# Block stores at a register's address in place of GpSimd scatters, for the first of four edge streams of a graph network

## The chip, the cores and the metric

One Trainium2 chip, one of its cores. The metric is the device time of one execution in microseconds (us), the median of several runs.

## The reference

Two layers of a relational graph convolution over 50,000 nodes of 128 features and 50,000 edges of 8 types, with `dst` sorted. Cut to what matters:

```python
h = relu(layernorm(x))
for l in range(2):
    m = relu(h[src] + edge_attr)                       # one message per edge
    seg = etype * n + dst
    mean = segment_sum(m, seg) / max(count(seg), 1)    # per (type, node)
    out = einsum('rnd,rdo->no', mean, weight[l])       # summed over the 8 types
    out = out + h @ root[l] + bias[l]
    h = batch_norm(out, gamma[l], beta[l])
    if l == 0: h = relu(h)
return x + h
```

`dst` is drawn as 50000 times the square of a uniform number and then sorted, so that the first edges lie close together in their nodes: the first quarter of the edges ends near node 3125.

## The kernel before

**Tiles, groups, streams.** The 50,000 edges, in order of dst, are cut into NT = 394 tiles of 127 edges. NG = 99 groups hold up to H = 4 tiles each, tile t belonging to group t % 99: stream 0 is tiles 0 to 98, stream 1 tiles 99 to 197 and so on. One group is one step of the edge loop, and there is one edge loop per layer.

**One step, group g.** GpSimd (POOL) gathers `h[src]` for each tile (`gather`, L759) into a ring of 20 groups (layer 0) or 9 (layer 1). VectorE (DVE) normalises it together with ScalarE (ACT) in layer 0, or scales it in layer 1, and adds the edge rows, which SyncE (SP) has loaded into `xb`, a ring of XB = 4 groups (`edge_rows`, L638; `edge_sum`, L1061 and L1067). TensorE (PE) transposes the tile (L1456) and spreads the edge types (L1463); ACT writes the message (L1265); DVE splits it by type (`by_type`, L1078); PE multiplies by the weights (`products`, L1481 and L1482, 8 products per tile); ACT copies the product (L1273); PE sums the edges of one node (`node_sums`, L1493); ACT copies the sums to `ob`, a ring of OB = 4 groups (`sums_out`, L1294), and row 0 of the sums to the next tile's input (`carry`, L1286). A tile's last node may go on in the next tile, so the sums of it are carried there.

**The scatters.** POOL writes each tile of `ob` to the table `acc[l]` in DRAM with an indirect DMA of 128 rows (`scatter`, L770). The row numbers are in `idx_t`; rows that hold no node's sum go to spare rows behind the table. Scatters and gathers alternate on POOL: `gathers_before` gives how many gathers lie ahead of the n-th scatter, 80 ahead in layer 0 and 36 in layer 1 at the start, 28 at the end. The first scatter of a group waits for `ob_ready` of that group. ACT waits for the scatters of group g-4 before it overwrites their slot of `ob`. When `dst` isn't sorted, a flag found during the set-up sends POOL, PE and DVE into a branch that works one scatter at a time; it isn't taken here.

**Order on the other queues.** PE's iteration i holds products(i), with types(i+2), turn(i+2) and node_sums(i-1) after its second tile. In layer 1, 44 of the iterations also hold four transposes (`first_rows`, L1503) and a product (`first_product`, L1508) of whole chunks of node rows, whose results are used after the loop. SP's iteration n loads the edge rows of group n, and in layer 0 loads and stores half chunks of normalised rows (L663, L652) and zeroes a part of `acc[1]` (L670); in layer 1, at n = 4i+2, it waits for the transposes of two chunks before (`ownT_ps`) and loads the next whole chunk (`table_dma`, L531). At the end of a layer, POOL adds three joined rows (`join_streams`, L795) once all scatters have landed, and SP then loads the sums chunk by chunk.

**Set-up.** DVE works out from `dst` and the types: whether dst is sorted (`falls`, `flag_i`), the scatter rows (`idx_t`), the slot of each edge's sum in its tile (`slot`, later `ikey_t`) and the inverse counts. ACT zeroes `acc[0]` meanwhile.

Of the kernel before, what the change touches and what calls it, by code (L numbers as in the profile page):

```python
# [41 lines left out]
def gnn_kernel(nc, x, src, dst, edge_attr, edge_type, weight, root, bias, gamma, beta, out):  # L42
# [70 lines left out]
    def tiles(g):  # L113
        return [s * NG + g for s in range(H) if s * NG + g < NT]

    ORDER = [(g, t) for g in range(NG) for t in tiles(g)]
    assert sorted(t for g, t in ORDER) == list(range(NT)) and tiles(0) == [s * NG for s in range(H)]

# [5 lines left out]
    with ctx:  # L124
# [48 lines left out]
        falls = sb("falls", [P, 1])  # L173
        goes_on = sb("goes_on", [P, NB])

        J = H - 1
# [139 lines left out]
        def own_at(i):  # L316
            return own_place[OWN_FIRST[i]]
# [134 lines left out]
        xb_in = [sem(f"xb_in{s}") for s in range(XB)]  # L452
        scat_out = [sem(f"scat_out{s}") for s in range(OB)]
        ve_ready = sem("ve_ready")
        sd_ready = sem("sd_ready")
# [112 lines left out]
        def tiles_done(gg, ring):  # L568

            return sum(len(tiles(k % NG)) for k in range(gg % ring, gg + 1, ring))  # L570

# [33 lines left out]
        def _(sp):  # L605
# [131 lines left out]
        def _(pool):  # L737
# [24 lines left out]
            def scatter(g, t, l, add):  # L762
                gg = l * NG + g
                if t == g:
                    pool.wait_ge(ob_ready, gg + 1)

                if t // NG == 2 and g + 4 < NG:
                    pool.wait_ge(tr_ps, gg + 5)
                how = {"compute_op": ALU.add, "bounds_check": N - 1, "oob_is_err": False} if add else {}
                pool.indirect_dma_start(out=acc[l], out_offset=at(idx_t[:, t:t + 1]), in_=ob[:, gg % OB, t // NG, :],  # L770
                                        in_offset=None, **how).then_inc(scat_out[gg % OB], 16)

            def scatter_alone(g, t, l):

                gg = l * NG + g
                j = t // NG
                if j > 0:
                    pool.wait_ge(scat_out[gg % OB], 16 * (tiles_done(gg, OB) - len(tiles(g)) + j))
                elif gg > 0:
                    pool.wait_ge(scat_out[(gg - 1) % OB], 16 * tiles_done(gg - 1, OB))  # L780
                scatter(g, t, l, True)

            def gathers_before(n, l):
# [62 lines left out]
        def _(dve):  # L846
# [28 lines left out]
            own.link(v.tensor_tensor_reduce(out=kill[:, :, 1:P], in0=dstf[:, :, 0:T], in1=dstf[:, :, 1:P], scale=1.0, scalar=0.0,  # L875
                                            op0=ALU.subtract, op1=ALU.max, accum_out=falls[:, 0:1]))
            own.link(v.tensor_scalar(falls[:, :], falls[:, :], 0.0, None, ALU.is_gt))
            dve.sem_inc(falls_ready, 1)


# [4 lines left out]
            own.mark(v.memset(agree[:, :, T:P], 0.0))  # L885
            own.mark(v.memset(keep[:, :, 0:1], 0.0))
            own.join()
# [5 lines left out]
            own.link(v.tensor_tensor(keep[:, :, :], kill[:, :, :], keep[:, :, :], ALU.mult))  # L893
            own.mark(v.tensor_tensor(kill[:, :, turned], keep[:, :, :], spare_row[:, :, :], ALU.add))

# [8 lines left out]
            dve.wait_ge(flag_ps, 1)  # L904
            v.tensor_scalar(flag_i[:, :], ps_s[0][0:1, 0:1], 0.5, None, ALU.is_gt).then_inc(flag_ready, 1)
            dve.wait_ge(cols_ps, 3)
# [311 lines left out]
        def _(act):  # L1218
# [426 lines left out]
```

## Time and profile before

| | |
|---|---|
| median of 3 runs | 2535.77 us (2532.77 to 2540.87) |
| span of the profiled execution | 3011.2 us |
| mean granted TensorE clock in it | 0.893 |
| PE, DVE, ACT, POOL busy | 2477.2, 1916.1, 969.3, 1603.3 us |
| edge loop of layer 0 | about 135 to 1309 us of the profiled execution |
| whole-chunk stage and batch norm of layer 0 | about 1310 to 1498 us |
| edge loop of layer 1 | about 1541 to 2745 us |
| stages behind it | about 2750 to 3011 us |

The profile is of one execution, and that one spans 3011.2 us, 475 us more than the median of the timed runs. Its durations are used below, but its total isn't that of a timed run. Times are counted from the span's start. "Idle before, <- X" is the time for which the engine did nothing ahead of the instruction, and X what ended it; "issue" means that the profile shows nothing that it waited for.

### The profile page before, as it was taken

The numbers are of one execution on the slowest core, as the hardware profiler recorded it, in microseconds if no ns is written. First come the engines' busy times: TensorE is split into PE (matmuls) and PEld (weight loads), VectorE is DVE, ScalarE is ACT, GpSimd is POOL, SyncE is SP. The second block draws the span as 40 slices with busy tenths as digits, with TensorE's granted clock in tenths as the row PEclk, the third lists the DMA queues.
The fourth block names the chain that finished last, engine by engine and source line by source line (L and its number), as shares of the span: only waits on it lengthen the run. The fifth ranks groups of instructions, "written<-read, shape, count | busy, mean of one in ns | idle before, by whom it ended". The sixth has DMA issues, their size and how long they took to land. (4 is left out here: it accounts for less than half of the span.)

```text
span 3011.2 us, 50450 instructions
## 1 busy us (share of the span) xinstructions
PE 2477.2 (82%) x19096; PEld 2315.6 (77%) x19096; DVE 1916.1 (64%) x5063; ACT 969.3 (32%) x2076; POOL 1603.3 (53%) x1613
## 2 busy tenths in 40 slices
PE   2388888888888888889968888898988889887976
PEld 1387887888787887789857878787888878777965
DVE  7566776777766667748855555565665556554754
ACT  0233344444444444424311222222222222222555
POOL 7566555665556555520056666666666666663000
PEclk7699998988998999999978999899999999988986
DMA  9533433344433333359922222222222222224889
GB/s 348 197 102 116 137 127 128 128 129 133 133 128 127 128 118 122 113 208 418 371 66 67 63 84 62 85 65 85 65 86 64 85 64 84 78 73 176 312 320 403
DMA packets 241842, 436.67 MB, mean 145 GB/s; under 512 B 39075, under 2 KB 144126, under 8 KB 241596
## 3 DMA queue, kind: packets, MB, share of 16 engines
q1 hardware_dynamic: 166134, 237.95, 22.6%
q0 software_dynamic: 53808, 115.45, 12.5%
q10 hardware_dynamic: 21654, 79.99, 6.6%
q8 instruction: 155, 2.54, 0.3%
q14 instruction: 91, 0.75, 0.1%
HBM read 255.41 MB, written 177.83 MB: 144 GB/s over the span
## 5 line engine op out<-in xcount | busy, mean ns | idle before, releaser
L1481 PE MATMUL ps_y<-arena 128*128 128x128 f32 x11032 | 1517.4, 287 | 227.9 <-issue 200.7
L1481 PEld LDWEIGHTS ps_y<-arena 128*128 128x128 f32 x11032 | 1412.1, 202 | 303.5 <-issue 278.5
L770 POOL DMA_INDIRECT acc<-arena x788 | 776.3, 985 | 728.1 <-ACT arena L1294 448.4
L1078 DVE SCALAR_TENSOR_TENSOR arena<-ps_s,arena 128x512 f32<-128x512 f32 (+1 forms) x1386 | 842.7, 678 | 362.9 <-PE ps_y L1482 186.0
L759 POOL DMA_INDIRECT arena<-h_rows,arena x394 | 411.9, 1045 | 300.3 <-DMA h_rows<-chunk_mem 180.5
L1273 ACT ACTIVATE arena<-ps_y 128x512 f32<-128x512 f32 (+1 forms) x198 | 117.9, 595 | 1259.8 <-remote 953.3
L759 POOL DMA_INDIRECT arena<-in_x_dram,arena x394 | 397.9, 1010 | 126.6 <-issue 118.9
L1482 PE MATMUL ps_y<-arena 128*128 128x128 f32 x1576 | 324.1, 286 | 23.2 <-issue 22.3
L1493 PE MATMUL ps_o<-arena 128*128 128x128 f32 x1576 | 260.8, 303 | 51.6 <-issue 49.0
L1493 PEld LDWEIGHTS ps_o<-arena 128*128 128x128 f32 x1576 | 226.8, 213 | 74.4 <-issue 73.0
L1482 PEld LDWEIGHTS ps_y<-arena 128*128 128x128 f32 x1576 | 254.0, 201 | 29.3 <-issue 29.1
L1265 ACT ACTIVATE arena<-ps_t 128x512 f32<-128x512 f32 (+1 forms) x198 | 115.5, 583 | 416.7 <-remote 310.9
L1090 DVE TENSOR_SCALAR arena<-arena 128x128 f32<-128x128 f32 x788 | 223.9, 352 | 0.0
L1049 DVE RECIPROCAL rstd<-sd 128x8 f32<-128x8 f32 (+2 forms) x99 | 19.6, 198 | 320.7 <-ACT arena L1257 227.2
L1456 PE MATMUL ps_t<-ident,arena 128*128 128x128 f32 x788 | 141.3, 300 | 51.7 <-issue 41.7
L1257 ACT ACTIVATE arena<-arena,nmr,rstd 128x128 f32<-128x128 f32 x394 | 160.8, 477 | 15.3 <-DVE nmr L1050 12.2
L1067 DVE SCALAR_TENSOR_TENSOR arena<-arena 128x512 f32<-128x512 f32 (+1 forms) x99 | 68.2, 689 | 142.6 <-DMA arena<-in_edge_attr_dram 134.5
L1456 PEld LDWEIGHTS ps_t<-ident,arena 128*128 128x128 f32 x788 | 94.8, 155 | 64.3 <-issue 53.8
L1463 PE MATMUL ps_s<-arena 128*128 128x128 bf16 x788 | 90.0, 235 | 37.8 <-issue 36.9
L1294 ACT ACTIVATE arena<-ps_o 128x512 f32<-128x512 f32 (+1 forms) x198 | 116.7, 589 | 2.7 <-PE ps_o L1493 2.7
L1286 ACT ACTIVATE arena<-ps_o 1x512 f32<-1x512 f32 (+1 forms) x196 | 111.4, 568 | 0.0
L1463 PEld LDWEIGHTS ps_s<-arena 128*128 128x128 bf16 x788 | 68.6, 108 | 40.7 <-issue 35.8
(230 smaller groups left out, 2251.7 us busy)
## 6 DMA issues: line engine op xcount, KB each, us to landing
arena<-in_edge_attr_dram SPq DMA_DIRECT2D x190, 256.0 KB
chunk_mem<-acc SPq DMA_DIRECT2D x55, 512.0 KB, 12.3
acc<-arena ACTq DMA_DIRECT2D x28, 896.0 KB
acc<-arena SPq DMA_DIRECT2D x28, 896.0 KB
arena<-in_x_dram SPq DMA_DIRECT2D x45, 512.0 KB, 9.8
arena<-acc SPq DMA_DIRECT2D x43, 512.0 KB, 10.1
chunk_mem<-hn_rows SPq DMA_DIRECT2D x41, 512.0 KB
out_dram<-arena ACTq DMA_DIRECT2D x38, 512.0 KB, 9.4
```

The costliest lines, as they stand in the source:

```text
L759: pool.indirect_dma_start(out=hb[:, hb_slot(gg), t // NG, :], out_offset=None, in_=(x, h1_tab)[l], in_offset=at(src_t[:, t:t + 1])).then_i ...
L770: pool.indirect_dma_start(out=acc[l], out_offset=at(idx_t[:, t:t + 1]), in_=ob[:, gg % OB, t // NG, :], in_offset=None, **how).then_inc(sc ...
L1078: ins = v.scalar_tensor_tensor(mk[:, m, r, 0:n], ps_type[gg % 2][:, 0:n], float(r), mt[:, gg % MT, 0:n], ALU.is_equal, ALU.mult)
L1090: ins = v.tensor_scalar(sm[:, gg % SM, c], iota_f[:, :], ikey_t[:, t:t + 1], inv_t[:, t:t + 1], ALU.is_equal, ALU.mult)
L1257: ins = a_.activation(row, row, ACT.Relu, scale=rstd[:, g % 2, j:j + 1], bias=nmr[:, g % 2, j:j + 1])
L1273: a_.activation(yb[:, gg % 2, 0:w, :].rearrange("p w d -> p (w d)"), ps_y[gg % 2][:, 0:w * D], ACT.Copy).then_inc(yb_ready, 1)
L1294: a_.activation(ob[:, gg % OB, 0:w, :].rearrange("p w d -> p (w d)"), ps_o[gg % 2][:, 0:w * D], ACT.Copy).then_inc(ob_ready, 1)
L1456: last = te.transpose(ps_turn[:, j * D:(j + 1) * D], hb[:, hb_slot(gg), j, :], ident[:, :])
L1463: last = te.matmul(bank[:, j * D:(j + 1) * D], ident_b[:, t % P:t % P + 1].to_broadcast([P, P]), rows_b[:, t // P, :], start=True, stop=True)
L1481: te.matmul(ps_y[gg % 2][:, c], mk[:, gg % MKS[l], r, c], w_sb[l][:, r * D:(r + 1) * D], start=r == 0, stop=False)
L1482: last = te.matmul(ps_y[gg % 2][:, c], mt[:, gg % MT, c], w_sb[l][:, (R - 1) * D:R * D], start=False, stop=True)
L1493: last = te.matmul(ps_o[gg % 2][:, c], sm[:, gg % SM, c], yb[:, gg % 2, j, :], start=True, stop=True)
```

## The change

Tiles 1 to 95 of stream 0 (one in each of the groups 1 to 95) are no longer scattered by POOL. For them the slot of a node's sum in `ob` is its distance from the tile's first node plus 1, and rows without a sum are zero, so that rows 1 to 112 of `ob` are 112 neighbouring rows of the table. SP writes them as one plain DMA, at an address that it loads into a register from `first_i`. A window reaches past its tile's last node and writes zeros there, so the windows go in order: each waits until the one before has landed, and the next window puts the right sums over the zeros. SP issues the window of group n-8 in its iteration n. ACT waits for the window, as it did for the scatter, before it overwrites the slot. The scatter of tile 96 and the join wait for the windows. Set-up gains the slots, the first rows and a test (`over`, `near_end`) that the tiles fit into windows; if not, the one-at-a-time branch is taken.

```diff
+    WROWS = 112
+    SPANS = ((1, NG - 4),)
+    WIDE = [t for a, b in SPANS for t in range(a, b + 1)]
@@ sync
+            def window_rows(g, l):
+                gg = l * NG + g
+                for t in in_window(g):
+                    sp.wait_ge(ob_ready, gg + 1)
+                    if gg > 0:
+                        wait(sp, wide_out, 16 * windows(gg - 1))
+                    first = sp.value_load(first_i[0:1, t:t + 1], min_val=0, max_val=P * (F + 1))
+                    sp.dma_start(acc[l][bass.ds(first, WROWS), :], ob[1:1 + WROWS, gg % OB, t // NG, :]).then_inc(wide_out, 16)
+
+            sp.wait_ge(idx_ready, 1)
             for l in range(L):
+                sp.wait_ge(acc_zero[l], 16 * ZN)
                 for n in range(NG):
                     if l > 0 or n >= 2:
                         edge_rows(n, l)
+                    if n >= 8:
+                        window_rows(n - 8, l)
...
+                for g in range(NG - 8, NG):
+                    window_rows(g, l)
@@ gpsimd, scatter
+                if not add and t in WIDE:
+                    return
+                if not add and t - 1 in WIDE:
+                    pool.wait_ge(wide_out, 16 * windows(gg - 1))
@@ gpsimd, join_streams
+                pool.wait_ge(wide_out, 16 * windows((l + 1) * NG - 1))
@@ vector, set-up
+            t0 = spare_row[:, 0:WB, 0]
+            own.mark(v.tensor_scalar(is_wide[:, :], t0, float(SPARE_ROW + P * SPANS[0][0]), None, ALU.is_ge))
+            own.mark(v.tensor_tensor(over[:, :], dstf[:, 0:WB, T], dstf[:, 0:WB, 0], ALU.subtract))
...
+            near = keep[:, 0:WB, :]
+            own.mark(v.tensor_tensor(agree[:, 0:WB, :], dstf[:, 0:WB, 0:P], dstf[:, 0:WB, T:P].to_broadcast([P, WB, P]),
+                                     ALU.not_equal))
+            own.link(v.tensor_tensor(near, dstf[:, 0:WB, 0:P], dstf[:, 0:WB, 0:1].to_broadcast([P, WB, P]), ALU.subtract))
+            own.link(v.scalar_tensor_tensor(near, near, 1.0, agree[:, 0:WB, :], ALU.add, ALU.mult))
+            own.link(v.tensor_tensor(near, near, slot[:, 0:WB, :], ALU.subtract))
+            for b in range(WB):
+                own.link(v.scalar_tensor_tensor(slot[:, b, :], near[:, b, :], is_wide[:, b:b + 1], slot[:, b, :],
+                                                ALU.mult, ALU.add))
...
+            own.link(v.tensor_scalar(first_i[:, :], dst_t[0:1, 0:WB * P], to_spare[:, 0:1], None, ALU.max))
@@ scalar, sums_out
                     act.wait_ge(scat_out[gg % OB], 16 * tiles_done(gg - OB, OB))
+                    wait(act, wide_out, 16 * windows(gg - OB))
```

## Rows read from the trace of the kernel before

**Rows 1.** The page, part 1: busy time and share by engine.
```profile
PE 2477.2 (82%) x19096; PEld 2315.6 (77%) x19096; DVE 1916.1 (64%) x5063; ACT 969.3 (32%) x2076; POOL 1603.3 (53%) x1613
```
**Rows 2.** Windows of both edge loops: length, busy per engine, granted clock, DMA share, GB/s.
```profile
135.58:1306.82 1171.24, 992.33 (x7788) 949.27 (x7786) 810.59 (x2860) 479.17 (x1190) 689.87 (x702) 0.92 0.37 123
1553.49:2739.33 1185.84, 1043.79 (x8050) 962.54 (x8048) 698.01 (x1350) 256.67 (x477) 760.39 (x746) 0.92 0.25 73
```
**Rows 3.** Timeline (start, length in us), ScalarE: first and last L1273 of the run.
```profile
135.58 0.60 ACT L1273 ACTIVATE arena<-ps_y 128x512 f32<-128x512 f32 x1 [2.88 <-PE ps_y L1482]
...
2739.33 0.49 ACT L1273 ACTIVATE arena<-ps_y 128x384 f32<-128x384 f32 x1 [4.26 <-PE ps_y L1482]
```
**Rows 4.** Timeline, ScalarE, end of layer 1: L1273 of two neighbouring groups.
```profile
2718.04 0.60 ACT L1273 ACTIVATE arena<-ps_y 128x512 f32<-128x512 f32 x1 [3.98 <-PE ps_y L1482]
...
2726.58 0.60 ACT L1273 ACTIVATE arena<-ps_y 128x512 f32<-128x512 f32 x1 [3.90 <-PE ps_y L1482]
```
**Rows 5.** Waits: who waited for whom, us in total, times, longest.
```profile
POOL acc L770 <- ACT arena L1294: 448.4, 147, 24.1
PE ps_y L1481 <- issue: 200.7, 311, 2.4
SPq L531 <- PE ps_t L1503: 765.0, 16, 63.2
```
**Rows 6.** Timeline, PE, layer 1: the product and the transposes of whole chunks.
```profile
1805.39 1.02 PE L1508 MATMUL ps_t<-ht,root_sb 128*128 128x512 f32 x2
1806.25 1.72 PE L1481 MATMUL ps_y<-arena 128*128 128x128 f32 x14
...
1816.80 0.60 PE L1503 MATMUL ps_t<-ident,arena 128*128 128x128 f32 x4
1817.24 1.73 PE L1481 MATMUL ps_y<-arena 128*128 128x128 f32 x14
```
**Rows 7.** The page, part 5: POOL's groups (busy, mean ns of one; idle before).
```profile
L770 POOL DMA_INDIRECT acc<-arena x788 | 776.3, 985 | 728.1 <-ACT arena L1294 448.4
L759 POOL DMA_INDIRECT arena<-h_rows,arena x394 | 411.9, 1045 | 300.3 <-DMA h_rows<-chunk_mem 180.5
L759 POOL DMA_INDIRECT arena<-in_x_dram,arena x394 | 397.9, 1010 | 126.6 <-issue 118.9
```
**Rows 8.** Timeline, POOL, layer 1: a scatter behind a gather.
```profile
2579.72 0.97 POOL L770 DMA_INDIRECT acc<-arena  x1 [0.30 <-issue]
```
**Rows 9.** Landings: SP's stores and loads in the timeline, and the join's in the chain.
```profile
81.03 0.35 SPq L645 DMA_DIRECT2D inv_rows<-chunk_mem  x1
89.35 0.37 SPq L647 DMA_DIRECT2D arena<-inv_rows  x1
...
1795.30 0.34 SPq L531 DMA_DIRECT2D arena<-h_rows  x1
1795.69 2.14 SPq L638 DMA_DIRECT2D arena<-in_edge_attr_dram  x4
...
2750.06 2.50 DMA acc<-join_sum,join_at
```
**Rows 10.** Timeline, DVE, layer 1: the edge sum that waits for edge rows.
```profile
1799.73 0.69 DVE L1067 SCALAR_TENSOR_TENSOR arena<-arena 128x512 f32<-128x512 f32 x1 [9.07 <-DMA arena<-in_edge_attr_dram]
```
**Rows 11.** Timeline, DVE, set-up: two small instructions, and the wait behind the flag.
```profile
7.99 0.23 DVE L868 TENSOR_SCALAR arena<-arena 128x128 f32<-128x128 f32 x1
13.73 0.15 DVE L877 TENSOR_SCALAR falls<-falls 128x1 f32<-128x1 f32 x1
77.81 0.55 DVE L1009 TENSOR_SCALAR chunk_mem<-chunk_mem 128x392 f32<-128x392 f32 x1 [8.61 <-issue]
```
**Rows 12.** Timeline, end of layer 1: SP's chunk loads, ACT's sums, PE's first chunk.
```profile
2672.13 41.76 SPq L531 DMA_DIRECT2D arena<-h_rows  x4
...
2727.08 0.59 ACT L1294 ACTIVATE arena<-ps_o 128x512 f32<-128x512 f32 x1
...
2758.24 1.91 PE L1546 MATMUL ps_t<-ident,arena 128*128 128x128 f32 x8
```

More of the change, by code:

```diff
@@ L114, in tiles, with listed, in_window, windows @@
         return [s * NG + g for s in range(H) if s * NG + g < NT]
+    WROWS = 112
+    SPANS = ((1, NG - 4),)
+    WIDE = [t for a, b in SPANS for t in range(a, b + 1)]
+    WB = WIDE[-1] // P + 1
+    assert all(a % NG > 0 and b % NG + 2 < NG and a // NG == b // NG for a, b in SPANS) and WROWS < P
+    def listed(g):
+        return [t for t in tiles(g) if t not in WIDE]
+    def in_window(g):
+        return [t for t in tiles(g) if t in WIDE]
+    def windows(gg):
+        return sum(len(in_window(k % NG)) for k in range(gg + 1))
     ORDER = [(g, t) for g in range(NG) for t in tiles(g)]
@@ L174, in gnn_kernel @@
         goes_on = sb("goes_on", [P, NB])
+        is_wide = sb("is_wide", [P, WB])
+        behind = sb("behind", [P, WB])
+        over = sb("over", [P, WB])
+        most = sb("most", [P, 1])
+        near_end = sb("near_end", [1, len(SPANS)])
+        to_spare = sb("to_spare", [1, 1])
+        first_i = sb("first_i", [1, WB * P], I32)
         J = H - 1
@@ L453, in gnn_kernel @@
         scat_out = [sem(f"scat_out{s}") for s in range(OB)]
+        wide_out = sem("wide_out")
         ve_ready = sem("ve_ready")
@@ L568, in tiles_done @@
         def tiles_done(gg, ring):
-            return sum(len(tiles(k % NG)) for k in range(gg % ring, gg + 1, ring))
+            return sum(len(listed(k % NG)) for k in range(gg % ring, gg + 1, ring))
         def out_count(c):
@@ L781, in scatter_alone @@
                 scatter(g, t, l, True)
+                if t in WIDE:
+                    pool.wait_ge(counted, 16 * (FE + l * len(WIDE) + sum(1 for _, k in ORDER[:ORDER.index((g, t)) + 1] if k in WIDE)))
             def gathers_before(n, l):
@@ L885, in _ @@
             own.mark(v.memset(agree[:, :, T:P], 0.0))
-            own.mark(v.memset(keep[:, :, 0:1], 0.0))
+            own.mark(v.memset(keep[:, WB:NB, 0:1], 0.0))
+            own.mark(v.tensor_tensor(keep[:, 0:WB, 0], keep[:, 0:WB, 0], behind[:, :], ALU.mult))
             own.join()
@@ L893, in _ @@
             own.link(v.tensor_tensor(keep[:, :, :], kill[:, :, :], keep[:, :, :], ALU.mult))
-            own.mark(v.tensor_tensor(kill[:, :, turned], keep[:, :, :], spare_row[:, :, :], ALU.add))
+            own.link(v.tensor_tensor(kill[:, :, turned], keep[:, :, :], spare_row[:, :, :], ALU.add))
+            near = keep[:, 0:WB, :]
[4 more added lines that the diff above has]
+            own.link(v.tensor_tensor(near, near, slot[:, 0:WB, :], ALU.subtract))
+            for b in range(WB):
+                own.link(v.scalar_tensor_tensor(slot[:, b, :], near[:, b, :], is_wide[:, b:b + 1], slot[:, b, :],
+                                                ALU.mult, ALU.add))
             own.link(v.memset(agree[:, :, :], BIG))
@@ L904, in _ @@
             dve.wait_ge(flag_ps, 1)
-            v.tensor_scalar(flag_i[:, :], ps_s[0][0:1, 0:1], 0.5, None, ALU.is_gt).then_inc(flag_ready, 1)
+            for k, (a, b) in enumerate(SPANS):
+                end = (b // NG + 1) * NG
+                own.link(v.tensor_tensor(near_end[:, k:k + 1], dst_t[0:1, end:end + 1], dst_t[0:1, b:b + 1], ALU.subtract))
+                own.link(v.tensor_scalar(near_end[:, k:k + 1], near_end[:, k:k + 1], float(WROWS), None, ALU.is_lt))
+            own.link(v.tensor_copy(most[0:1, :], ps_s[0][0:1, 0:1]))
+            for k in range(len(SPANS)):
+                own.link(v.tensor_tensor(most[0:1, :], most[0:1, :], near_end[:, k:k + 1], ALU.max))
+            own.mark(v.tensor_scalar(flag_i[:, :], most[0:1, :], 0.5, None, ALU.is_gt))
+            own.mark(v.tensor_scalar(to_spare[:, :], most[0:1, :], 0.5, float(SPARE_ROW), ALU.is_gt, ALU.mult))
+            own.join()
+            dve.sem_inc(flag_ready, 1)
+            own.link(v.tensor_scalar(first_i[:, :], dst_t[0:1, 0:WB * P], to_spare[:, 0:1], None, ALU.max))
             dve.wait_ge(cols_ps, 3)
```

21 lines of the change are left out of this document (17 added, 4 removed).

## The prediction

> **What bounds the kernel now.** I read the busy shares first [rows 1]: TensorE (PE) is busy for 82% of the profiled span, GpSimd (POOL) for 53%, VectorE for 64%, ScalarE for 32%. Then the two edge loops (one per layer) by themselves [rows 2]: together 2357 of 3011.2 us. The reader is to see that PE works for 85% and 88% of them while the DMA engines are busy for 37% and 25%, so bytes are not the limit. The change lives in these loops and in the set-up ahead of them, so I look for what sets the step from one group of tiles to the next.
>
> The profiled execution spans 3011.2 us and the median of the timed runs is 2535.8 us. The timed runs are 475 us shorter, more than any edit here could move, so I first have to say where the profiled execution spends those 475 us. One ScalarE instruction per group (L1273) shows the step. The two windows are cut at its first and last start in each layer [rows 2, 3]: 1171.24 and 1185.84 us, 98 steps each, so 11.95 and 12.10 us. At the end of layer 1, where gathers have stopped, the same step is 2726.58 - 2718.04 = 8.54 us [rows 4], and there PE has no hole. Elsewhere PE loses time to "issue", which is time in which it waited for nothing that the profile shows; 200.7 us stand at L1481 alone [rows 5]. So PE's own floor is 8.54 us in layer 0. In layer 1 it has 44 extra half chunks: four transposes take 1817.24 - 1816.80 = 0.44 us and a product 1806.25 - 1805.39 = 0.86 us [rows 6]. 44 x 1.30 = 57 us, 0.58 us per step, floor 9.12 us.
>
> Now the timed runs. Outside the loops the profiled execution spends 3011.2 - 2357.1 = 654 us. If that is the same without a profiler, the timed loops take 2535.8 - 654 = 1882 us, 9.60 us per step. PE's floor gives 196 x 8.54 + 57 = 1731 us, a run of 2385 us. So 151 us of the timed run are not PE's floor.
>
> POOL's pace explains them. A scatter (L770) is 0.985 us and the gathers (L759) 1.010 us in layer 0 and 1.045 us in layer 1 [rows 7]; 0.30 us lie between two of them even where it waits for nobody [rows 8]. A group has 4 scatters, and the formula of the lead gives 314/366 and 358/366 gathers per scatter, so 3.43 and 3.91. POOL needs 4 x 1.285 + 3.43 x 1.31 = 9.63 us in layer 0 and 4 x 1.285 + 3.91 x 1.345 = 10.40 us in layer 1. In the profiled execution that is less than the step of 12 us, and POOL waits once or so a group for ScalarE's L1294 (448.4 us in all) [rows 5]. With PE's holes gone it is more than PE's floor: 92 steps each give 1843 us, 12 steps at the ends 102 us, and with the 654 us a run of 2599 us. The measured 2535.8 lies between 2385 and 2599 and nearer to POOL's number. I take POOL as the pacemaker of the timed runs, at (1882 - 102)/1843 = 0.966 of its profiled duration, so 9.30 and 10.05 us per step.
>
> **The change part by part.**
> *Scatters removed.* Tiles 1 to 95, one per group, in both layers: 190 of 788. Each is 1.285 x 0.966 = 1.24 us of POOL. Its pace falls to 8.06 and 8.80 us, under PE's 8.54 and 9.12. PE then ends last, and the gain stops there: 0.76 + 0.93 = 1.69 us, x 92 = 155 us. POOL (8.06), VectorE (810.59/98 = 8.27 us busy per step in layer 0 [rows 2]) and PE (8.54) are then so close that they will not interlock without loss; no row shows this price. Its ends are 0 (the bare step [rows 4]) and 0.76 us (no gain in layer 0). I take 0.25 us, nearer to the bare step since that one also has POOL scattering: 184 x 0.25 = 46 us lost.
>
> *Windows on SyncE (SP).* Each iteration of SP's loop gets a wait for ob_ready, a wait that the previous window has landed, a register load and a DMA of 112 rows (57 KB). Behind these waits in SP's queue stand the edge rows of later groups, the early half chunks in and out, and the own loads. Edge rows are loaded four groups ahead, more than one step of slack, so I cost the wait for ob_ready at nothing; if that cover were gone, VectorE would wait at L1067 as it already does once in four groups of layer 1 (9.07 us) [rows 10]. The window's landing: nearest rows are 2.50 us (the join's scatter at the end of the layer) and 8.32 us less 0.35 us of issue (SP's store of the inverse counts, with the DMA engines saturated) [rows 9]. I take 4 us, from the edge rows that were issued at 1795.69 and released VectorE at 1799.73 [rows 9, 10]. The register load has no row of its own; it lies inside VectorE's 8.61 us of idle time after the flag, which also holds a branch [rows 11], so its ends are 0 and 8.61 us; I take 1 us, near the short end, because PE, POOL and SP have short gaps everywhere else. The Trainium skill, "Runtime: NRT & Kernel Launch", Instruction fetch mechanics, speaks of about 200 ns per register loaded from memory; by that the cycle below would be 0.8 us shorter. Cycle of one window: 1 + 0.4 + 4 = 5.4 us, under the step of 9 us.
>
> *Where SP itself is late.* In layer 1 SP's queue stands at L531 for the transposes of L1503, 765.0 us in all [rows 5], and then sends the own load and four edge loads in one burst [rows 9]. The window of group 4i-5 is now in that burst, and ScalarE may not overwrite its buffer (L1294) for group 4i-1 before it has landed. From the end of L1503: 0.67 us to SP's issue, 0.34 own load, 0.5 edge rows, 1 register, 0.4 issue, 4 landing, 1.2 for ScalarE's two copies, 8.1 us; PE wants the carried row (L1286) after four tiles of products (4 x 1.79) and 0.67 us, so after 7.8 us. I take 0.9 us lost 20 times: 18 us. With a landing of 2.5 us it is nothing, with 8 us it is 4.3 x 20 = 86 us.
>
> *Set-up.* About twenty small VectorE instructions on the chain that leads to the inverse counts: thirteen of [128 x 1] or [1 x 1] at 0.15 us plus a semaphore each, 0.2 us, and six of [128 x 128] at about 0.23 us [rows 11], 4 us. If the saturated DMA hides it, 0. Waits of SP for acc_zero and idx_ready: SP already stands for the inverse counts until 81.03 us, and POOL needs the same zeros; at nothing.
>
> *Layer ends.* Groups 96 to 98 keep all their scatters, so the last POOL scatters and the join stay where they are. SP's first chunk loads now stand behind window 95, whose sums are ready at about 2728 us; the loads took off from 2672 us before [rows 12]. They need about 10 us and PE uses them at 2758 us, so they stay covered, and cost some 5 us if they did not.
>
> *Bytes.* 112 instead of 127 rows of 512 B, 190 times: nothing, with the DMA at 25 to 37%.
>
> *Sum.* -155 + 46 + 18 + 4 = -87 us. 2535.8 - 87 = 2449 us. On the profiled execution itself the sum is different, since POOL is not its pacemaker: 3011.2 + 4 + 18, less whatever of PE's holes goes with the scatters; about 3000 us.
>
> **The rivals.**
> *A: POOL is not the pacemaker of the timed runs* (PE's holes remain in part without a profiler). For it: the profile shows PE's holes and POOL waiting [rows 5]. Against it: 475 us are gone in the timed runs. Then nothing is gained and set-up costs 4 us: 2540 us; with the 18 us of layer 1, 2558 us.
> *B, on the slow side: SP's one-at-a-time chain becomes the clock.* Each window waits for the landing of the one before, and ScalarE waits for the window four groups back. It decides from a cycle of 9.3 us (layer 0) and 10.05 us (layer 1). With the upper ends of both unknown prices the cycle would be 17 us. At 10.5 us it costs (1.2 + 0.45) x 95 = 157 us: 2693 us. Against it: the DMA engines are busy for a third only [rows 2]. The Trainium skill, "DMA: Bandwidth & Descriptors", Anatomy of one DMA, gives a fixed 2.0 us per transfer whatever its size, which is the rule against serial small transfers; by it the cycle would be shorter than mine, and the 2.50 us of rows 9 agree.
> *C: the list is found unfit* (a tile of stream 0 spans more than 112 nodes) and the kernel takes its one-at-a-time branch, far above 3000 us. The first quarter of the edges has at least two edges per node by the square law of dst, so 127 edges span some 64 nodes at most; chance 0.01.
> *D: full gain.* No interlock loss and no stall in layer 1: 2535.8 - 155 + 4 = 2385 us.
>
> **How the numbers follow.** Forecast 0.62 (2400 to 2520 us), D 0.05, A 0.20 (of which two thirds within 0.3%), B 0.12, C 0.01. The range leaves out about 0.05 below and 0.13 above: 2395 to 2560 us. About 0.3%, 7.6 us, is what a measurement of this kernel can tell from no change. Faster 0.67, same 0.13, slower 0.20.
>
> **What would show it.** POOL's L770 count falls from 788 to 598. POOL's wait for L1294 grows (it is early), by about 1.3 us per group. In the timed runs the loss is 80 to 90 us. A ScalarE wait before L1294 for a DMA once in four groups of layer 1 would show the stall, and one in every group would show B. A doubling of window landings beyond 4 us, or an unchanged time with POOL relieved, would make the forecast wrong.

## The result

The changed kernel takes 2361.52 us (2359.79 to 2363.17), the kernel before beside it 2535.8 us (2532.77 to 2540.87): the ratio is 0.931, 95% interval 0.930 to 0.932. That is 174 us less. The forecast was 87 us less, and the time lies below the range.

The profiled execution of the changed kernel spans 2357.9 us, so this time the profile and the timed runs agree. The page, part 1 and three lines of part 5, answers to [rows 1] and [rows 7]; the lines of the code have moved (L770 is now L816, L759 L801, L1273 L1360, L1294 L1382, L1481 L1569, L1503 L1591, L1067 L1154).

```profile
PE 2189.4 (93%) x19096; PEld 2130.4 (90%) x19096; DVE 1913.6 (81%) x5084; ACT 972.6 (41%) x2076; POOL 1415.2 (60%) x1423
...
L816 POOL DMA_INDIRECT acc<-arena x598 | 608.0, 1017 | 226.5 <-issue 172.1
L801 POOL DMA_INDIRECT arena<-h_rows,arena x394 | 391.0, 992 | 307.1 <-DMA h_rows<-chunk_mem 179.7
L801 POOL DMA_INDIRECT arena<-in_x_dram,arena x394 | 399.1, 1013 | 154.6 <-issue 103.9
```

788 scatters have become 598, and PE is busy for 93% of the span. The windows of the two loops and of two stretches within them, in the columns of [rows 2]:

```profile
110.39:959.89 849.50, 848.37 (x7788) 846.90 (x7788) 809.28 (x2864) 479.29 (x1189) 610.50 (x616) 1.00 0.55 168
1179.79:2084.53 904.74, 904.70 (x8050) 882.36 (x8048) 696.91 (x1354) 260.20 (x477) 675.32 (x666) 1.00 0.33 96
...
500.00:800.00 300.00, 300.00 (x2758) 299.60 (x2757) 295.61 (x1070) 177.27 (x445) 219.80 (x223) 1.00 0.60 182
1500.00:1900.00 400.00, 400.00 (x3550) 389.31 (x3549) 308.97 (x600) 117.00 (x214) 303.84 (x300) 1.00 0.34 100
```

PE is busy for 848.37 of 849.50 us in layer 0 and for 904.70 of 904.74 us in layer 1: there is no hole left. The step is its own, as the starts of L1360 in the timeline of ScalarE show (two in layer 0, then five in layer 1):

```profile
608.38 0.60 ACT L1360 ACTIVATE arena<-ps_y 128x512 f32<-128x512 f32 x1 [3.51 <-PE ps_y L1570]
617.09 0.60 ACT L1360 ACTIVATE arena<-ps_y 128x512 f32<-128x512 f32 x1 [3.51 <-PE ps_y L1570]
...
1606.61 0.60 ACT L1360 ACTIVATE arena<-ps_y 128x512 f32<-128x512 f32 x1 [4.31 <-PE ps_y L1570]
1616.17 0.60 ACT L1360 ACTIVATE arena<-ps_y 128x512 f32<-128x512 f32 x1 [4.73 <-PE ps_y L1570]
1625.31 0.60 ACT L1360 ACTIVATE arena<-ps_y 128x512 f32<-128x512 f32 x1 [4.30 <-PE ps_y L1570]
1634.88 0.60 ACT L1360 ACTIVATE arena<-ps_y 128x512 f32<-128x512 f32 x1 [4.73 <-PE ps_y L1570]
1644.02 0.60 ACT L1360 ACTIVATE arena<-ps_y 128x512 f32<-128x512 f32 x1 [4.31 <-PE ps_y L1570]
```

8.71 us in layer 0, and (1644.02 - 1606.61)/4 = 9.35 us in layer 1, where steps of 9.14 and 9.57 us alternate: each pair of steps holds four transposes and one product of whole chunks besides.

One thing has to be said before any comparison of traces. The kernels were run on several chips, and on some of them the same kernel before takes 2980 to 3020 us (its ratios are therefore taken only within one chip). The profiled execution shown ahead of the prediction, 3011.2 us, looks like one from such a chip, while the timed runs beside it do not. What differs is told in the last section. The experiments of the later section on chips of the slow kind are read as ratios; the decisive runs were made where the kernel before takes 2535 us.

### The profile page after: what moved, and what is told of

Same layout as the page of the kernel before. It is cut to its first block and busy times, and to the rows that moved or that the text cites. A ratio compares the mean times of both kernels' runs of the same rounds, so it can differ in the third digit from the quotient of the medians.

```text
span 2357.9 us, 51658 instructions
## 1 busy us (share of the span) xinstructions
PE 2189.4 (93%) x19096; PEld 2130.4 (90%) x19096; DVE 1913.6 (81%) x5084; ACT 972.6 (41%) x2076; POOL 1415.2 (60%) x1423
## 5 line engine op out<-in xcount | busy, mean ns | idle before, releaser
L1569 PE MATMUL ps_y<-arena 128*128 128x128 f32 x11032 | 1364.3, 275 | 4.2 <-DVE arena L1165 4.2
L1569 PEld LDWEIGHTS ps_y<-arena 128*128 128x128 f32 x11032 | 1302.1, 192 | 25.9 <-issue 21.0
L816 POOL DMA_INDIRECT acc<-arena x598 | 608.0, 1017 | 226.5 <-issue 172.1
L801 POOL DMA_INDIRECT arena<-h_rows,arena x394 | 391.0, 992 | 307.1 <-DMA h_rows<-chunk_mem 179.7
L801 POOL DMA_INDIRECT arena<-in_x_dram,arena x394 | 399.1, 1013 | 154.6 <-issue 103.9
L1360 ACT ACTIVATE arena<-ps_y 128x512 f32<-128x512 f32 (+1 forms) x198 | 117.8, 595 | 794.2 <-PE ps_y L1570 790.7
L1570 PE MATMUL ps_y<-arena 128*128 128x128 f32 x1576 | 304.9, 275 | 0.0
L1570 PEld LDWEIGHTS ps_y<-arena 128*128 128x128 f32 x1576 | 239.5, 192 | 0.0
L1581 PE MATMUL ps_o<-arena 128*128 128x128 f32 x1576 | 208.5, 275 | 2.7 <-issue 2.7
L1581 PEld LDWEIGHTS ps_o<-arena 128*128 128x128 f32 x1576 | 191.6, 192 | 3.0 <-issue 3.0
L1154 DVE SCALAR_TENSOR_TENSOR arena<-arena 128x512 f32<-128x512 f32 (+1 forms) x99 | 68.2, 689 | 93.0 <-DMA arena<-in_edge_attr_dram 90.3
L1544 PE MATMUL ps_t<-ident,arena 128*128 128x128 f32 x788 | 121.7, 277 | 11.0 <-DVE arena L1148 5.6
L1382 ACT ACTIVATE arena<-ps_o 128x512 f32<-128x512 f32 (+1 forms) x198 | 116.8, 590 | 22.9 <-DMA acc<-arena 20.9
L1708 PE MATMUL ps_t<-ident,arena 128*128 128x128 f32 x304 | 63.6, 372 | 34.7 <-ACT arena L1478 25.4
L1544 PEld LDWEIGHTS ps_t<-ident,arena 128*128 128x128 f32 x788 | 84.0, 142 | 12.0 <-DVE arena L1148 6.1
L1708 PEld LDWEIGHTS ps_t<-ident,arena 128*128 128x128 f32 x304 | 50.2, 196 | 47.9 <-ACT arena L1478 45.9
L1551 PE MATMUL ps_s<-arena 128*128 128x128 bf16 x788 | 77.2, 221 | 15.2 <-DVE arena L1108 14.6
```

What stands on the lines that cost most here:

```text
L801: pool.indirect_dma_start(out=hb[:, hb_slot(gg), t // NG, :], out_offset=None, in_=(x, h1_tab)[l], in_offset=at(src_t[:, t:t + 1])).then_i ...
L1360: a_.activation(yb[:, gg % 2, 0:w, :].rearrange("p w d -> p (w d)"), ps_y[gg % 2][:, 0:w * D], ACT.Copy).then_inc(yb_ready, 1)
L1544: last = te.transpose(ps_turn[:, j * D:(j + 1) * D], hb[:, hb_slot(gg), j, :], ident[:, :])
L1569: te.matmul(ps_y[gg % 2][:, c], mk[:, gg % MKS[l], r, c], w_sb[l][:, r * D:(r + 1) * D], start=r == 0, stop=False)
L1570: last = te.matmul(ps_y[gg % 2][:, c], mt[:, gg % MT, c], w_sb[l][:, (R - 1) * D:R * D], start=False, stop=True)
L1581: last = te.matmul(ps_o[gg % 2][:, c], sm[:, gg % SM, c], yb[:, gg % 2, j, :], start=True, stop=True)
```

## The kernel before, profiled where it takes 2535 us

> The kernel before, unchanged, profiled beside the others of this job. On chips with stretches of TensorE instructions 0.71 us apart it took 2970 to 3020 us, on the chip of the result 2535.8 us. Theory 1 (POOL's pace) on a chip without such stretches: steps of 9.63 and 10.40 us by POOL's profiled durations, 582 us outside the loops as in the changed kernel's trace, 2535 us. With them: as before.

The kernel before, unchanged: 2535.48 us, profiled span 2533.7 us, beside runs of 2534.51 us (2528.52 to 2539.48). This is the trace that the prediction lacked. Windows of its loops (first to last L1273) and of two stretches:

```profile
109.03:1047.26 938.23, 877.34 (x7788) 869.01 (x7788) 810.06 (x2866) 486.66 (x1189) 709.31 (x713) 0.98 0.47 154
1268.58:2257.26 988.68, 931.31 (x8050) 898.50 (x8048) 700.31 (x1351) 259.44 (x478) 758.71 (x756) 0.98 0.30 88
...
500.00:800.00 300.00, 280.26 (x2489) 276.98 (x2488) 264.44 (x960) 163.54 (x403) 229.93 (x231) 0.98 0.49 164
1500.00:1900.00 400.00, 371.13 (x3167) 356.61 (x3166) 276.46 (x531) 104.45 (x190) 306.81 (x307) 0.97 0.29 87
```

The loops take 938.23 + 988.68 = 1926.9 us instead of the 2357 of [rows 2], 9.57 and 10.09 us per step on average. In the first stretch POOL starts 231 instructions in 300 us, one per 1.299 us, and in the second 307 in 400 us, one per 1.303. That is the price of [rows 7, 8] (0.99 + 0.30) with nothing in between. The waits of that kernel in those stretches (500 to 800 us, then 1500 to 1900 us) say the same, with who waited, for whom, us in total, times and longest:

```profile
ACT arena L1294 <- DMA acc<-arena: 62.6, 21, 7.0
POOL acc L770 <- issue: 37.1, 122, 0.3
POOL arena L759 <- issue: 32.3, 106, 0.3
...
DVE arena L1064 <- DMA arena<-h_rows,arena: 120.0, 35, 7.4
POOL acc L770 <- issue: 47.2, 155, 0.3
POOL arena L759 <- issue: 46.0, 151, 0.3
ACT arena L1294 <- DMA acc<-arena: 30.2, 14, 4.9
```

Nearly all of POOL's idle time in these stretches is its own 0.3 us; it waits for nobody, and in the whole trace only 14.8 us at L770 for L1294, whereas in [rows 5] it was 448.4 us. The others wait for POOL: VectorE for a late gather (L1064), ScalarE for a late scatter to free its buffer (L1294). The bound is an engine busy for 77% of these stretches (229.93 of 300 us) and for 63% of the whole span.

It isn't the bound of every step. Behind a first step of 10.9 us, steps 2 to 32 of layer 0 are 8.7 us long, and the first 20 of layer 1 are those of PE too (8.7, then 9.14 and 9.57 us in turn): there POOL's head start is being used up, and PE sets the pace. POOL already issues without a pause in them, 209 instructions from 109 to 380 us, one per 1.297. A step holds 7.43 of its instructions in layer 0, 9.66 us, so POOL falls behind by 0.95 us per step, some 30 us in 32 steps. A scatter may be four groups late, 35 us, before ScalarE has to wait for it. That this is the room that runs out in layer 0 is worked out and not tested by a run; the first long waits behind it are ScalarE's at L1294. After that the steps are uneven, 8.7 to 15.5 us in layer 0, up to the short ones at the end of the loop.

## Experiments where the kernel before takes 2535 us

**One scatter per group left out, nothing put in its place.** In `scatter`, of the kernel before (`tiles_done`, which counts scatters for the waits, leaves the same tiles out):

```
+                if 1 <= t <= NG - 4:
+                    return
```

> The kernel before with one scatter per group left out, beside the changed kernel on one chip: its distance to the changed kernel is what windows and set-up cost. On the chip of the second job it was 55 us (2779 and 2834 us). Theory 1 on a chip without stretches: within 10 us.

2357.93 us (2357.3 to 2361.87), ratio 0.931 (0.929 to 0.933). Beside it the changed kernel again:

> The changed kernel unchanged, beside the kernel before on this chip. Theory 1: 6 to 7% faster than the kernel before, whichever kind of chip it is (0.931 with the result, 0.936 in the second job).

2361.59 us (2360.31 to 2362.57), ratio 0.932 (0.930 to 0.934). So taking away the work of POOL is worth 177 us, and all that the change puts in its place (190 windows, their waits, register loads and set-up) costs 3.7 us together. The two kernels' runs overlap (2357.3 to 2361.87 and 2360.31 to 2362.57), so it is not sure to be more than nothing.

**Two scatters per group left out.** The same edit, with the counts that go with it, for tiles 1 to 95 and 100 to 194; their sums go nowhere.

```
+                if t < 2 * NG and 1 <= t % NG <= NG - 4:
+                    return
```

> The kernel before with two scatters per group left out instead of one (tiles 1 to 95 and 100 to 194 of each layer; their sums go nowhere). GpSimd has 1.28 us per group less than with one left out, which gave 2358 us. Theory (after one scatter per group is gone, TensorE's floor of 8.7 and 9.35 us is the bound, so the gain ends there): 2355 us, ratio 0.93. Rival (GpSimd still sets the pace after the first, and the gain of 174 us is simply the GpSimd time removed): another 190 x 0.92 = 175 us less, 2183 us, ratio 0.861. If the two engines still interlock with loss after the change (my 0.25 us per step), 2358 - 46 = 2312 us, ratio 0.912.

2359.04 us (2357.69 to 2361.69), ratio 0.930 (0.928 to 0.932). The second scatter gives nothing: 2359 against 2358 us. The gain had ended at PE's floor with the first. The interlock loss of 0.25 us per step that I had priced would have given 2312 us; it isn't there.

**One of the eight products per tile left out, before and after the change.** In the loop of products into ps_o:

```
-                for r in range(R - 1):
+                for r in range(R - 2):
```

> The kernel before, with one of the eight products per tile into ps_o left out in both layers (the sums lack one basis). TensorE's work per group of four tiles falls by about 0.34 us. Theory (GpSimd sets the pace of both loops of the kernel before, once its lead is used up, and TensorE's holes are its): the time stays at that of the kernel before, 2536 us, ratio 0.995 to 1.0. Rival 1 (TensorE is the pacemaker before as well, and the change gains by something else): 196 x 0.34 = 66 us less, 2470 us, ratio 0.974. Rival 2 (both share the pace, since the ring of buffers couples them): half of it, 2503 us, ratio 0.987.

> The changed kernel, with one of the eight products per tile into ps_o left out in both layers (the sums lack one basis). Theory (with 190 scatters gone from GpSimd, TensorE's own work sets the step): 66 us less than the changed kernel's 2362, so 2296 us, ratio 0.905 to the kernel before. Rival (GpSimd, at 8.68 and 9.35 us per step, or SyncE's windows set the step after the change): the time stays at 2362 us, ratio 0.931.

The kernel before: 2526.11 us (2521.39 to 2529.18), ratio 0.995 (0.993 to 0.997), 12 us. The changed kernel: 2301.22 us (2298.09 to 2303.2), ratio 0.907 (0.905 to 0.909), 60 us less than the 2361.5. One cut, five times the gain once POOL is relieved. The two profiled executions (2533.7 and 2527.4 us) differ by 6.3 us, and 5.6 of these lie in the loop of layer 0 (938.23 and 932.59 us), 1.0 in that of layer 1. Which steps give them was not looked into.

The size that I expected for the cut was wrong: it takes 8 matmuls out of a group, and the step at the start of the loop falls from 8.70 to 7.8 us, 0.9 us and not 0.34. PE's floor alone would have given about 196 x 0.87 = 170 us. That only 60 came, close to the 66 that I had written, is a coincidence, and the trace shows why it stopped there. Timeline of VectorE in layer 0 of the changed kernel with one product less, two neighbouring steps:

```profile
610.26 0.76 DVE L1148 TENSOR_TENSOR arena<-arena 128x512 f32<-128x512 f32 x1
610.94 1.10 DVE L1177 TENSOR_SCALAR arena<-arena 128x128 f32<-128x128 f32 x4
611.96 0.85 DVE L1119 BATCH_NORM_STATS2 st<-arena 128x6 f32<-128x128 f32 x4
612.75 0.84 DVE L1124 BATCH_NORM_STATS2 st<-spare 128x6 f32<-128x128 f32 x4
613.62 0.64 DVE L1128 BATCH_NORM_AGGREGATE mv<-st 128x2 f32<-128x6 f32 x8
614.30 0.17 DVE L1130 TENSOR_SCALAR ve<-mv 128x8 f32<-128x8 f32 x1
614.41 4.27 DVE L1165 SCALAR_TENSOR_TENSOR arena<-ps_s,arena 128x512 f32<-128x512 f32 x7
618.60 0.19 DVE L1136 RECIPROCAL rstd<-sd 128x8 f32<-128x8 f32 x1
618.83 0.17 DVE L1137 SCALAR_TENSOR_TENSOR nmr<-mv,rstd 128x8 f32<-128x8 f32 x1
618.91 0.69 DVE L1148 TENSOR_TENSOR arena<-arena 128x512 f32<-128x512 f32 x1
```

VectorE has no gap from 610.26 to 618.91: it needs 8.65 us for this group by itself (most steps of this stretch are 8.6 us), and PE now waits for it. In layer 1 the third engine comes next; waits of the same kernel between 1500 and 1900 us:

```profile
DVE arena L1151 <- DMA arena<-h_rows,arena: 81.0, 40, 4.3
POOL arena L801 <- issue: 52.7, 173, 0.3
POOL acc L816 <- issue: 40.2, 132, 0.3
```

POOL again waits for nobody and VectorE for its gathers. With three scatters, POOL needs (3 + 3.91) x 1.303 = 9.0 us per group; the mean step of this layer is 8.9 us. So the changed kernel is balanced to a hair: 8.70 (PE) and 8.65 us (VectorE) in layer 0, 9.35 (PE) and 9.0 us (POOL) in layer 1.

## Experiments on chips of the slow kind

These came first and are weaker, since the engines have stretches of slow issue here. Kernel before on this chip: 2980.0 us (2975.62 to 2982.5).

> The kernel before, unchanged, profiled once more. It tells whether TensorE's holes in the edge loops (200.7 us before L1481 put down to issue, steps of 11.95 and 12.10 us) are the kernel's or the profiled execution's. Theory 1 (POOL sets the pace of the timed runs, the holes are an accident of that one profile): span near 2535 us, steps of POOL's length, about 9.6 us in layer 0 and 10.3 us in layer 1, no holes put down to issue. Theory 2 (the holes come with the profiler whenever POOL issues all of its 8 DMAs per group): span near 3011 us again, while the timed run is 2536 us.

2968.71 us with a profiled span of 2966.9 us: the profiler adds nothing, and the 475 us between the profiled execution and the timed runs of the case are not its doing.

> The kernel before with the 95 scatters per layer of stream 0 (tiles 1 to 95) left out and nothing in their place, so these rows of the result are missing; SP, set-up and ScalarE are as before. Theory 1 (POOL's relief is the whole gain and the windows cost nothing): 2355 to 2365 us, the time of the changed kernel. Rival (the windows or the set-up cost something, or bring something of their own): the difference from 2361.5 us is their price; by the prediction's terms for SP in layer 1 and the set-up it would be 22 us faster, 2340 us.

2734.13 us (2722 to 2745), ratio 0.917 (0.913 to 0.920), 246 us less. In the trace of the kernel before on this chip POOL waits 380.9 us for L1294 (134 times), so there it is not the engine that never waits. Why relieving it brings even more here isn't shown.

**The change, with POOL's scatters put back.** POOL also scatters tiles 1 to 95 to a table that nobody reads, and the waits for scatters count them again (cut to the scatter):

```
+                    pool.indirect_dma_start(out=aside, out_offset=at(idx_t[:, t:t + 1]), in_=ob[:, gg % OB, t // NG, :],
+                                            in_offset=None).then_inc(scat_out[gg % OB], 16)
```

> The changed kernel with POOL's load put back: SP still writes the windows, and POOL also scatters the same 95 tiles per layer into a table of its own that nobody reads; ScalarE waits for both. Theory 1 (POOL's pace): back to 2536 us within 10. Rival (the gain came from something else in the change: SP's order, the set-up, fewer rows): stays near 2362 us.

3019.57 us, ratio 1.013 (1.011 to 1.016). Windows on SP and scatters on POOL together bring nothing: on this kind of chip too, the gain goes with the 190 instructions that POOL no longer has. The run was not made where the kernel before takes 2535 us; there the scatter left out says the same.

> The kernel before with one of the eight products per tile left out (type 6's), so that the result lacks that type. TensorE has 4 x 2 instructions less per group, 4 x 0.22 = 0.9 us of its floor of 8.54 us. Theory 1 (POOL's pace in the timed runs): unchanged, 2536 us within 8. Rival A of the prediction (TensorE with holes sets the pace): 198 x 0.9 = 175 us faster, 2360 us.

2928.2 us, ratio 0.983 (0.982 to 0.985): 52 us, more than the 12 of the other kind of chip. Here PE, with its holes of slow issue, shares the pace; the run doesn't separate the theories.

On another chip (kernel before 3019.23 us, 3011 to 3032) the changed kernel:

> The changed kernel unchanged, beside the kernel before on one chip. In the last job's chip the kernel before took 2980 us with holes in TensorE's work put down to issue, against 2535.8 us on the chip of the result. Theory 1 (POOL's 8 DMAs per group are the pacemaker only on a chip without the holes, and the holes add to it on the other): 2362 us where before takes 2536; where before takes 2980, the changed kernel gains as much as the left-out scatters did there, about 2740 us. Theory 3 (the holes come from POOL being saturated, so the changed kernel has none anywhere): 2362 us on either chip.

2834.22 us (2808 to 2848), ratio 0.936 (0.930 to 0.942).

> The kernel before with the 95 scatters per layer left out and nothing in their place, again, now beside the changed kernel on one chip, so that the difference of the two is the price of windows and set-up. Theory 1: within 10 us of the changed kernel. By the prediction's terms for SP in layer 1 and the set-up: 22 us faster than the changed kernel.

2778.72 us, ratio 0.920 (0.917 to 0.923). What the change puts in place costs 55 us here against 3.7 us above. Over half of it lies ahead of the loops: the first L1360 of the changed kernel starts at 166.31 us, the same instruction of the other at 136.59. The set-up with its many small VectorE instructions costs 29.7 us here. Where the kernel before takes 2535 us, the same two kernels reach that instruction at 110.17 and 109.48 us, 0.7 us apart. Where the other 25 us go wasn't settled.

> The changed kernel with one of the eight products per tile left out (type 6's), so that the result lacks that type; TensorE's floor per step falls by 0.9 us. Theory 1 (TensorE sets the pace now, POOL is 0.3 to 0.4 us per step behind it): on a chip without holes 0.3 to 0.5 us per step faster, 60 to 90 us, 2275 to 2300 us, then POOL's pace. If POOL weren't next: 175 us faster, 2187 us. With holes: less than 60 us, as before's 52 us.

2753.97 us (2729 to 2764), ratio 0.910 (0.902 to 0.918), 80 us less than the changed kernel, whose own runs spread over 40 us; before the change the same cut gave 52 on the other chip.

**Each window written four times, one after the other**, to make SP's chain longer (cut to the loop; the other waits for windows count four for one):

```
+                    for q in range(WX):
+                        if q:
+                            sp.wait_ge(wide_out, 16 * (WX * windows(gg) - WX + q))
+                        sp.dma_start(acc[l][bass.ds(first, WROWS), :], ...).then_inc(wide_out, 16)
```

> The changed kernel with each window written four times, one after another, each waiting until the last has landed; POOL and TensorE as in the changed kernel. In the changed kernel's trace one window's cycle in a burst of layer 1 is 2.4 us (SP issues at 1516.19 and 1518.56). Theory 1 (SP's chain is far from being the clock): a cycle of about 9.2 us is still about the step of 8.7 to 9.35 us, so up to 60 us slower than the changed kernel. Rival B of the prediction (the chain is near the clock already): over 300 us slower.

2921.31 us, ratio 0.968 (0.964 to 0.972), 87 us more than the changed kernel. The line of its waits at SP for the window before:

```profile
SPq L693 <- DMA acc<-arena: 353.7, 227, 3.9
```

353.7/227 = 1.6 us each, never more than 3.9. Three further landings per group, some 5 us more in SP's chain, lengthen a group by only 87/190 = 0.46 us: the chain of single windows has nearly all of that to spare, even where everything issues slowly.

On a third chip (kernel before 2982.71 us) four of these were repeated for their spread:

> The kernel before, unchanged, a third profile. The runs so far were on chips on which TensorE's sequencer has stretches of one instruction in 0.71 us where it has 0.112 us otherwise (172 to 235 such instructions in layer 0's loop at one line alone), and on which this kernel takes 2980 to 3020 us; the changed kernel's profile with the result has one such instruction. If this chip has none: theory 1 (POOL's pace) says about 2536 us, steps of 9.6 us in layer 0 and 10.3 us in layer 1, and POOL never waits for ScalarE's L1294 in the loops. If it has them again: 2970 to 3020 us as before, which tells nothing new.

> The changed kernel with POOL's load put back (it also scatters the 95 tiles per layer into a table that nobody reads). Theory 1 (POOL's pace is the whole difference): the time of the kernel before within 1%, where the changed kernel is 6.9% faster. On the chip with holes it was 1.3% over the kernel before.

> The kernel before with one of the eight products per tile left out (type 6's), so that the result lacks that type; TensorE's floor is 0.9 us per step lower. Theory 1 on a chip without holes: POOL sets the pace, within 8 us of the kernel before. Rival A (TensorE sets it): 175 us faster. With holes it was 52 us faster.

> The changed kernel with one product per tile left out (type 6's), so that the result lacks that type. Theory 1 on a chip without holes: TensorE set the pace, now POOL does, at 3 scatters and 3.43 or 3.91 gathers of 1.28 us per step, 8.3 and 9.0 us where the steps were 8.7 and 9.35: 0.4 + 0.35 us over 92 steps, 70 us faster than 2362, 2292 us. If POOL weren't next, 175 us faster, 2187 us.

2970.52 us; 3000.22 us, ratio 1.006 (1.004 to 1.009); 2931.99 us, 0.983 (0.981 to 0.985); 2704.87 us, 0.904 (0.899 to 0.909). The same picture: POOL's scatters put back undo the gain. With one product less the changed kernel is at 0.904, where without the cut it was 0.936 on the chip before (it wasn't run on this one); the kernel before gains 0.017 by the same cut.

## Why the prediction was half of the gain

**Right: the bound and its place.** POOL was the pacemaker of the timed runs, by its issue rate and not its busy share. Read from a trace in which PE was the one with holes [rows 5], this rested on the sum alone; the trace above confirms it, and so do the two cuts of PE. That the gain stops at PE's floor is shown by the second scatter, which gave nothing. Of the signs named, the count of L770 fell to 598, and rival A falls with the trace and the two cuts. The wait of POOL for ScalarE's copy of the sums was to grow by about 1.3 us per group. It grew from 14.8 to 29.6 + 57.1 = 86.7 us (at L816 and at L801), 0.4 us per group, since POOL with 6.43 instructions of 1.30 us needs 8.36 of the 8.71 us.

**Wrong, the largest term: the 654 us outside the loops.** They were taken from the profiled execution of 3011.2 us and subtracted from a median of other runs. In the trace of 2533.7 us the loops leave 2533.7 - 1926.9 = 606.8 us, and in that of the changed kernel 603.7 (the 582 in the expectation above is a slip). With 607 the prediction's own step reads 2535.8 - 607 = 1929 us in the loops, POOL's scale (1929 - 102)/1843 = 0.991 and not 0.966, its pace 9.55 and 10.31 us and not 9.30 and 10.05. The relief down to PE's 8.54 and 9.12 is then (1.01 + 1.19) x 92 = 202 us and not 155: 47 us of the 87 that were missed. The 0.966 had no mechanism behind it, since it said that POOL would be faster in the timed runs than its own instructions in the trace. That was the warning.

**Wrong in kind: the interlock.** 46 us were taken off for three engines that are close to one another. Nothing is lost to that: PE runs 400.00 of 400 us, and one step of layer 0 is as long as the next, 8.70 or 8.71 us. What there is instead is a floor higher than the bare step of [rows 4]: 8.70 and 9.35 us instead of 8.54 and 9.12, (0.16 + 0.23) x 92 = 36 us. The last groups have three tiles, so PE spreads the types of one tile less and transposes one tile less in the bare step. The timeline of PE shows it, in a step of layer 0 and then in the bare one:

```profile
611.75 0.39 PE L1551 MATMUL ps_s<-arena 128*128 128x128 bf16 x4
611.98 0.61 PE L1544 MATMUL ps_t<-ident,arena 128*128 128x128 f32 x4
...
2058.54 0.33 PE L1551 MATMUL ps_s<-arena 128*128 128x128 bf16 x3
2058.70 0.50 PE L1544 MATMUL ps_t<-ident,arena 128*128 128x128 f32 x3
```

From the start of the first to the start of what follows (612.42 and 2059.04) are 0.67 and 0.50 us, and the 0.17 between them is the difference of the steps. A step at the end of a loop is a poor measure of those within. In layer 1 there is the same 0.16, and 0.07 more: the 44 half chunks lie in 88 steps that follow one another, so they cost 1.30/2 = 0.65 us per step and not 0.58, spread over 98. 10 us of the difference.

**Wrong: the stall in layer 1.** The mechanism is there as foretold, at ScalarE, once in four groups; its price at the end of the run is nothing. Nor did the 18 us follow from the working: the chain of 8.1 us against 7.8 makes 0.3 us, 20 times, 6 us, and the 0.9 us stood without a source. Timeline of SP in layer 1 and of ScalarE beside it, then the waits of the changed kernel:

```profile
1509.49 0.33 SPq L557 DMA_DIRECT2D chunk_mem<-h_rows  x1
1509.87 0.44 SPq L664 DMA_DIRECT2D arena<-in_edge_attr_dram  x1
1511.13 0.34 SPq L688 DMA_DIRECT2D acc<-arena  x1
1511.51 0.62 SPq L664 DMA_DIRECT2D arena<-in_edge_attr_dram  x1
1516.19 0.34 SPq L688 DMA_DIRECT2D acc<-arena  x1
1516.57 0.43 SPq L664 DMA_DIRECT2D arena<-in_edge_attr_dram  x1
1518.56 0.34 SPq L688 DMA_DIRECT2D acc<-arena  x1
...
1520.97 0.34 SPq L688 DMA_DIRECT2D acc<-arena  x1
...
1515.52 0.60 ACT L1382 ACTIVATE arena<-ps_o 128x512 f32<-128x512 f32 x1 [1.85 <-DMA acc<-arena]
```

```profile
DVE arena L1154 <- DMA arena<-in_edge_attr_dram: 90.3, 20, 5.5
ACT arena L1382 <- DMA acc<-arena: 20.9, 20, 2.2
```

The burst after the own load is the one described: own load, edge rows, window. From the window's issue at 1511.13 to the copy that it releases are 4.39 us, where I had put 0.4 + 4. ScalarE loses 1.0 us in each of 20 groups. But PE has no hole in this stretch, so the carried row arrives in time: the chain that I ended at "PE wants the carried row after 7.8 us" has a little more room than the 0.3 us by which I had it late. 18 us of the difference. The wait at L1154 that I had named as the danger is in the row above it, 20 times as in the kernel with one scatter left out (91.5 us, 20), which has no windows; so it isn't theirs, and PE hides it too.

**Right: what costs next to nothing.** In the burst a window goes out every (1520.97 - 1516.19)/2 = 2.39 us: wait, register load, issue and landing together, against my 5.4. The register load has a row in this trace, with its shortest, median and longest time in ns:

```profile
L687 SPq TENSOR_LOAD <-first_i x190: 262/268/487, 130.3 to 2073.4; - x190
```

From the start of the load to the window's issue the median is 0.70 us, since checks and the address come behind it, where I had 1. That leaves 1.7 us from a window's issue to the start of the next load, landing included, against my 4.4. The Trainium skill, "DMA: Bandwidth & Descriptors", Anatomy of one DMA, puts the fixed part of a transfer that GpSimd issues at 2.0 us. SyncE's windows in the burst took less, and the first one, in the crowd, 4.39 us to the copy that it released, so the measurement decides. Rival B was never near. The set-up moved VectorE's L1009 of [rows 11] (L1096 now) from 77.91 us in the trace of 2533.7 us to 80.97, and SP's store of [rows 9] from 81.00 to 84.05 us: 3.1 us. Of these 1.4 are left at the first L1360 (110.39 against 109.03 us); I had 4.

**The sum again.** 202 - 36 = 166 us is what the loops should have lost by this. In the two traces they lost 938.23 - 849.50 = 88.7 and 988.68 - 904.74 = 83.9 us, 172.7 together. The other 7 us are at the starts and ends of the loops, or in POOL's own pace; this was not settled. Ahead of the loops 1.4 us are lost, and between and behind them the changed kernel is 4.4 us shorter, for no reason that was looked for. That makes 176 us between the traces, and 174 in the timed runs.

| term, us | predicted | measured |
|---|---|---|
| relief of POOL down to PE's bare step | 155 | 202 (worked out again with 607 us outside) |
| interlock; in its place a higher floor | -46 | -36 |
| stall in layer 1 | -18 | 0 |
| set-up | -4 | -1 |
| between and behind the loops | 0 | 4 |
| left over in the loops | | 7 |
| total | 87 | 176 (timed runs: 174) |

Rival D (full gain, 2385 us, chance 0.05) had it right that neither interlock nor stall costs anything. It missed by the same 654 us.

## What to carry to other kernels

If the profiled execution and the timed runs are hundreds of microseconds apart, take no term by difference between them: let the pacemaker's own durations carry the sum, and if a scale below 1 is needed to make them fit, look for the wrong subtrahend. The engine that sets the pace can be one that is busy for 63%; count its instructions per step, with the gap between them. Close engines need not cost an interlock loss: here, with buffers four groups deep, 8.70 us of PE beside 8.65 of VectorE and 8.36 of POOL lost nothing. The gain of relieving one engine ended sharply at the next one's floor, which is read within the loop and not at its end.

## What the runs showed of the hardware

The same kernel took 2535 us beside the result and on the chip of the last experiments, and 2980 to 3019 us (medians) on three others, in every run there. The traces of the slow kind have stretches in which an engine starts its next instruction late though the profile shows nothing that it waits for. Waits for "issue" at the product L1569 and at VectorE's L1136, changed kernel on a chip of the slow kind (span 2846.3 us), and what the changed kernel's trace of 2357.9 us has for PE at its product L1581:

```profile
PE ps_y L1569 <- issue: 157.8, 240, 3.2
DVE rstd L1136 <- issue: 97.0, 36, 6.2
```

```profile
PE ps_o L1581 <- issue: 2.7, 2, 1.4
```

PE and VectorE showed them above all, in the set-up too. The word alone doesn't mark them: the kernel before has 36.0 us of it at L1493 in the trace of 2533.7 us as well, behind ScalarE's copies that waited for late scatters. They stayed with one product or one scatter less (L1569: 99.5 us with one product less; L1483, the same line: 140.7 us with the scatter left out). What causes them stays open; no kernel here was made to find out. The relative gain of the change was about the same on both kinds (0.931, and 0.936 with an interval of 0.930 to 0.942).

Of TensorE's clock: with holes in the kernel before, its granted clock in the loops was 0.98 of 2.4 GHz and the same 7788 matmuls of layer 0 kept it busy for 877.34 us; with none it was 1.00 and 848.37 us. With one product less, and so more holes, it was 0.94 and 0.96. The clock accounts for about 2% of 848 us, 17 of the 29 us (an estimate); what makes up the rest isn't shown. No term of mine held this, but the step of 8.70 us is measured with the clock at 1.00.
